# A decoder layer on one core: the output products of the scan slots stand behind the scores of three key blocks instead of four

## The reference, cut to what matters

```
x = x + attn(layernorm(x))          # 16 heads of 32, 2 key-value heads, causal
    scores = einsum(Qg, K) / sqrt(32); masked; softmax; times V
    return out @ Wo + bo            # the output products
x = x + scan(ctx, layernorm(x))     # state = state * exp(dt*A) + (dt*u)*B; y = state . C
                                    # 4 batches, 16 states, 512 channels, 512 steps
x = x + moe(layernorm(x))
```

## Time and profile before

| | |
|---|---|
| profiled execution | 1143.58 us |
| its span in the trace | 1141.9 us |
| median of 3 runs | 1143.83 us |
| PE busy / PEld busy | 94% / 59% of the span |
| DVE, ACT, POOL busy | 73%, 59%, 59% |
| mean granted clock of PE | 0.985 of full speed |
| first and last scan | 142.7 and 650.1 us |
| output matmuls L865 | 192 instructions, first at 292.9 us |

### The profile page before, as it was taken

How to read it: one execution, slowest core, us unless ns; L and a number is a source line. 1 busy time by engine, 2 the same in 40 slices (tenths; PEclk the granted TensorE clock), 3 DMA queues, 4 the chain that set the end, 5 groups by cost and what they waited for, 6 DMA issues and landing times.

```text
span 1141.9 us, 19309 instructions
## 1 busy us (share of the span) xinstructions
PE 1072.3 (94%) x6746; PEld 676.3 (59%) x6746; DVE 832.3 (73%) x1245; ACT 676.6 (59%) x1467; POOL 677.9 (59%) x587
## 2 busy tenths in 40 slices
PE   8999989888999999999999977999999999999994
PEld 3554456666667666766666743444444477777761
DVE  6998699999999999999999998640680144443438
ACT  4876789999999999999999835202011022233220
POOL 2112399999999999999999871102043045555530
PEclk9999989999999999999999998999999999999997
DMA  7310011112111121111221053102225534444229
GB/s 222 93 38 20 21 29 38 38 39 66 38 35 32 34 70 38 30 37 30 84 67 38 11 186 111 74 37 74 74 74 204 174 93 135 132 135 133 72 79 385
DMA packets 51983, 94.77 MB, mean 83 GB/s; under 512 B 9966, under 2 KB 18158, under 8 KB 51888
## 3 DMA queue, kind: packets, MB, share of 16 engines
q1 hardware_dynamic: 44368, 72.82, 20.2%
q0 software_dynamic: 7520, 20.72, 5.9%
HBM read 74.51 MB, written 20.84 MB: 84 GB/s over the span
## 4 chain that ended last, share of the span: by engine, by line
PE 69%; ACT 9%; POOL 8%; DVE 7%; issue 5%; DMA 2%; SPq 0%; DVEq 0%; POOLq 0%; ACTq 0%
PE ps L1516 10%; PE ps L1939 7%; PE ps L1951 7%; PE ps L823 6%; PE ps L1530 5%; POOL w_all L758 4%; PE ps L851 4%; PE ps L356 4%; PE ps L812 4%; PE ps L797 4%; PE ps L865 3%; PE ps L308 3%; ACT w_all L934 3%; PE ps L1539 2%; ACT ps L917 2%
## 5 line engine op out<-in xcount | busy, mean ns | idle before, releaser
L758 POOL TENSOR_TENSOR w_all<-w_all 128x512 f32<-128x512 f32 x256 | 320.8, 1273 | 22.1 <-DVE w_all L585 14.8
L1013 DVE TENSOR_TENSOR_SCAN w_all<-ps,w_all 128x512 f32<-128x512 f32 x256 | 299.1, 1206 | 1.7 <-POOL w_all L758 1.1
L917 ACT ACTIVATE ps<-w_all,low 128x512 f32<-128x512 f32 x256 | 176.9, 695 | 1.0 <-DVE w_all L1013 0.8
L851 PE MATMUL ps<-ident,w_all 128*128 128x128 f32 x1024 | 161.8, 281 | 6.6 <-DVE acc L1021 6.5
L925 ACT ACTIVATE w_all<-ps,low 128x128 f32<-128x128 f32 (+3 forms) x256 | 132.7, 529 | 13.2 <-DVE low L1005 13.2
L851 PEld LDWEIGHTS ps<-ident,w_all 128*128 128x128 f32 x1024 | 113.9, 141 | 31.3 <-issue 18.2
L1450 POOL TENSOR_TENSOR w_all<-w_all 128x512 f32<-128x512 f32 x24 | 29.4, 1225 | 147.9 <-ACT w_all L1651 147.9
L1989 DVE COPY attn<-w_all 128x512 f32 x94 | 40.1, 428 | 103.7 <-PE ps L1939 102.8
L1005 DVE TENSOR_REDUCE low<-ps 128x2 f32<-128x256 f32 (+3 forms) x128 | 103.9, 812 | 13.9 <-PE ps L797 13.5
L1516 PE MATMUL ps<-w_all 128*128 128x512 f32 x256 | 113.3, 598 | 0.0
L934 ACT ACTIVATE w_all<-ps 128x256 f32<-128x256 f32 (+2 forms) x192 | 101.7, 530 | 17.0 <-PE ps L812 16.6
(11 more groups left out here) (218 smaller groups left out, 1713.9 us busy)
## 6 DMA issues: line engine op xcount, KB each, us to landing
w_all<-b_scratch SPq DMA_DIRECT2D x64, 256.0 KB, 3.3
w_all<-in_w_up SPq DMA_DIRECT2D x16, 512.0 KB, 6.2
w_all<-in_w_down SPq DMA_DIRECT2D x16, 512.0 KB, 7.0
w_all<-sorted_y SPq DMA_DIRECT2D x16, 512.0 KB, 9.7
norms<-attn SPq DMA_DIRECT2D x4, 1024.0 KB, 4.3
out_dram<-acc SPq DMA_DIRECT2D x16, 256.0 KB, 9.4
attn<-in_x SPq DMA_DIRECT2D x3, 1024.0 KB, 6.2
attn<-in_x SPq DMA_DIRECT2D x12, 256.0 KB, 4.5
```

Of the source, the lines that this page charges most:

```text
L758: pool.tensor_tensor(dbu[:, k, :], keep["du"][i // N][:, k * T:(k + 1) * T], b_all[i % 2][:, :], ALU.mult).then_inc(pool_dbu.sem, pool_dbu ...
L851: last = pe.transpose(yb[which][:, k * P:(k + 1) * P], state[i % 2][:, k, t * P:(t + 1) * P], ident[:, :])
L917: act.activation(da[unit % 2][:, :], keep["dt"][i // N][:, k * T:(k + 1) * T], ACT.Exp, scale=keep["a_flat"][:, unit % (N * KD):unit % (N ...
L1013: dve.tensor_tensor_scan(state[i % 2][:, k, :], da[unit % 2][:, :], dbu[:, k, :], 0.0, ALU.mult, ALU.add).then_inc(dve_scan.sem, dve_scan. ...
```

## The change: where the outputs stand

```diff
     OUTS = 2 * NT * (B - 1)
-    FIRST_OUT = 8 * NT + NT + 2
+    FIRST_OUT = 8 * NT + NT + 1
```

## The result

The changed kernel takes 1169.22 us (median of 5 runs, 1168.97 to 1169.9), the kernel before 1143.83 (1143.11 to 1144.23). The ratio is 1.0224, with a 95% interval of 1.0212 to 1.0236; 25.4 us are lost. The prediction was 1171.8 us, in a range of 1157 to 1182. The medians in this document leave out one run, of the experiment with both side effects taken back, which took 1191.27 us at a mean clock of 0.938 where its three fellows had 0.98 to 0.988 and 1164.75 to 1167.77 us.

The account below looks back on a forecast made before the run. PE's work ahead of the four-block scores was taken to set the slot. Growths of 19.8 and 10.0 us, less 5.3 given back, plus 3.5 for ACT, make 28.0; with 1143.58 and 0.25, 1171.8 us (range 1157 to 1182).

Parts of the forecast that it names:

- The rival that by the share of weight loads PE has room: PEld busy only 22.31 of 32.23 us, so the output's loads fit and the time stays within 0.2%; chance 4%.
- Step 1 and 2: Slot 69: ACT scales before its copy, which ends at 418.10; PE's second probability transposes wait for it, 0.40 us later.
- Step 3: Slot 69, PE: the output goes behind the second group of probability transposes and takes 1.93 us.
- Steps 4 to 6: PE's 0.25 us wait for ACT disappears; L823 starts 2.08 us later; mask to reduce 1.38 us; slot 70 grows 1.65 us.
- step 4: The 0.25 us for which PE waited for ACT before L823 disappears under the output.
- step 2: PE's second group of probability transposes in slot 69 waits for ACT's copy and starts 0.40 us later.
- The spread's slot: Slot 66, with spread and four-block scores: the reduce moves from 406.90 to 407.81, so the slot grows by 0.91 us.
- the 0.69 us of ACT's order: Spread slots took 5.93 us with an output, 5.24 without, because ACT scaled before copying the spread; the change removes this.
- Given back 0.46: Slots behind fall to their lengths without outputs: at most 0.46 us a period, 0.23 per output, 5.3 us in all.
- ACT's lag: ACT's scaling in slot 70 comes late, delaying the next exponents: between 0 and 0.35 us an output, taken as 0.15.
- The sum: 12 x 1.65 and 11 x 0.91, less 5.3 given back, plus 3.5 for ACT: 28.0 us.
- The signs: Changed profile: period about 34.7 us, engines idle 3 us or more, slot 70's reduce waiting 1.9 us, slot 71 3.2 us.

Follow-up runs that it names:

- both side effects taken back: Changed kernel with ACT's scaling by C in its usual place and the second state transpose ahead of the scores again: 1166.06 us, ratio 1.0199.
- half outputs: 23 of 24 output products summed over two of four contraction blocks: changed kernel 1149.7 us, kernel before 1139.87 us.
- The transpose taken back: Changed kernel with the second state transpose of the slot behind an output ahead of the scores again on PE: 1170.47 us, ratio 1.0236.
- The other two places: Kernel before with outputs moved behind the scores of one key block (1160.18 us) or of two key blocks (1167.2 us).

## Why the prediction was right, point by point

**What bounds the kernel.** That PE's row ahead of the four-block scores sets the slot is shown by the half outputs (19.5 us in the changed kernel, 3.7 in the one before) and by both side effects taken back (a period of 34.24 us, where the changed kernel has 34.37). The rival that by the share of weight loads PE has room is refuted: PEld is busy for 22.42 of 34.37 us, 65%, in a kernel that waits for PE for 1.64 us in one slot.

**Step 1 and 2, ACT's scaling ahead of the copy: 0.40 us.** Measured at L812: 0.44 in slot 69 (3.01 to 3.45 us after the slot) and 0.32 in slot 65 (3.07 to 3.39), and 0.38 where it was done alone. Right.

**Step 3, the output: 1.93 us.** Too large. From L812 to the transpose L851 it was 0.49 and is 2.22 now: 1.73 us. The 1.93 was the interval from the output to the product with V. The starts of the single instructions show what it held beside the output's own time: its first step takes 0.32 us there and 0.22 now, and from its last instruction to the product with V it is 0.31, to the transposes 0.22. Eight instructions at about 0.215 us are 1.72.

**Steps 4 to 6.** The wait of 0.25 us is gone; L823 now starts 0.53 us behind the transpose (429.73, 430.26) where I had left 0.60. The mask stands in the transpose's place, and from mask to reduce it is 1.38 us as before. Slot 70 grew by 1.36 us (4.58 to 5.94) where I had 1.65; step 3 is 0.20 of the 0.29 and step 4 is 0.07. Slot 69 took 0.06 us of the delay, and step 2 was 0.04 longer than forecast, which leaves the other 0.02.

**The spread's slot: 0.91 us.** Measured 0.64 (5.93 to 6.57). The path through ACT's copy is as described (the last matmul of L834, the copy, 0.70 us to the normalize, 0.61 to the reduce); the same 0.20 and 0.07 us of steps 3 and 4 are what was too much. That the 0.69 us of ACT's order came back is seen against the lengths without outputs: both kinds of slot stand 1.36 us above them now (6.60 for 5.24, 5.94 for 4.58).

**Given back 0.46, ACT's lag 0.30 in a period.** The net of the other six slots was forecast at -0.16 us and is about +0.1: they were 0.46 above the lengths without outputs, now they are 0.57 above. The transpose taken back shows that these 0.57 us are ACT's lag alone: there the exponents start on time again, and PE's catching up is indeed given back in full, and every slot has its length without outputs. The lag is 0.28 us an output, not 0.15, yet within the bounds of 0 and 0.35.

**The sum.** Forecast 2.40 us a period, measured 2.14. With the sizes as measured, 12 x 1.36 + 11 x 0.64 + 11.5 x 0.11 = 24.6 us, which is what the trace has between slots 36 and 127. The two growths were 0.29 and 0.27 us too large, mostly by the output's size, and the net of the other slots 0.27 too small by the lag's: two misses of opposite sign, of which about half cancels. With the growths as measured and the lag as forecast the sum would have given 1165.4 us, with the lag as measured and the growths as forecast 1174.9. Both lie in the range, but that 1171.8 came within 2.6 us of the median is in part luck.

**The signs.** Those named for the changed profile are there, except two sizes: the reduce of slot 70 waits 1.64 us where 1.9 was forecast, and PE stands still for 2.74 us of the period (34.37 less 31.63), not for 3 or more. Slot 71 takes 3.33 us where 3.2 was named, and slot 67 takes 3.43: the lag was larger than taken, as the forecast said that this would mean.

**The clock.** 1.00 in the window after as before, with PE busy for 92% of it.

## What to carry to other kernels

In this kernel, whose engines run fixed rows and meet at semaphores, the best of four places for a block of work on the fullest engine was straight behind the result that keeps the other engines busy longest. There it lies beside what they do with it; one place earlier it stands ahead of that result and costs its whole length. The other two places show that the four-block scores are not the only result that counts: what costs is the next thing that any engine wants from PE. To see which of the two holds in another kernel, shorten the block in both places: a cut that is worth five times as much in one as in the other says more than any busy share. And when two waits end nearly together, removing the one that the trace names moves nothing; look for the next.

## What was not expected

The same eight instructions of an output take a different time to the next instruction on PE: 1.93 us in slot 70 before, 1.82 us in slot 66 before, 1.73 us in slot 69 after. The product with V follows in the first two. The weight loads of the output in slots 70 and 66 before:

```profile
422.06 1.59 PEld L865 LDWEIGHTS ps<-w_all,attn 128*128 128x128 f32 x8 [0.76 <-issue]
406.47 1.60 PEld L865 LDWEIGHTS ps<-w_all,attn 128*128 128x128 f32 x8
```

In slot 70 the first load starts together with the first matmul (422.06 for both), and the step to the second matmul is 0.32 us. In slot 66 before and slot 69 after, the load starts 0.11 us ahead (406.47 and 406.58, 427.89 and 428.00), and the step is 0.22, as all later ones are. So it is with all 23 outputs of both traces: 0.32 us in the twelve that stand straight behind the four-block scores, 0.22 in the eleven of the kernel before that stand behind transposes and in all of the changed kernel. The product with V adds 0.09 us in the same manner: its load, too, starts only with its matmul (423.99), while that of the transposes starts 0.21 us ahead (429.52 and 429.73). So in these traces such a group costs about 0.1 us more where its first weight load does not start ahead of its first matmul. Why it does not at these places is open.

A change of order on ACT by one place of 0.6 us made PE's transposes 0.38 us later, and this travelled over PE and back to ACT and DVE in full, 0.38 us for each of 23 outputs, though ACT is busy for only 92% of the period and DVE for 94%.
